# A gated cross-attention and sparse-FFN kernel on one core: direct factor writes, new instruction orders, a halved last tile

## What is computed

```python
x = x + tanh(g_xattn[0]) * xattn(layernorm(x), ctx, mask)
x = x + tanh(g_ffn[0]) * ffn(layernorm(x), w_gate, w_up, w_down)
...
def ffn(x, w_gate, w_up, w_down):
    h = silu(x @ w_gate) * (x @ w_up)        # 512 -> 2048
    h = keep_two_largest_of_each_four(h)     # by absolute value
    return h @ w_down                        # 2048 -> 512
```

## Time and profile before

| | |
|---|---|
| median of 3 runs | 1099.13 us (1098.95 to 1099.48) |
| the profiled execution | 1101.32 us, span 1099.5 us |
| PE busy | 1074.1 us (98%), 4960 matmuls |
| DVE, ACT, POOL busy | 796.6, 614.1, 222.2 us |
| mean granted PE clock | 0.995 |
| DMA | 254.75 MB, mean 232 GB/s |

### The profile page before, as it was taken

One profiled execution on the slowest core, in us unless ns is written; L12 is line 12 of the kernel. 1 busy time (PEld: TensorE's weight loads), 2 busy tenths in 40 slices (PEclk: granted clock), 3 DMA queues, 4 the chain that ended last, 5 costly groups with the idle time before them and its releaser, 6 DMA issues.

```text
span 1099.5 us, 15140 instructions
## 1 busy us (share of the span) xinstructions
PE 1074.1 (98%) x4960; PEld 879.7 (80%) x4960; DVE 796.6 (72%) x1391; ACT 614.1 (56%) x1126; POOL 222.2 (20%) x340
## 2 busy tenths in 40 slices
PE   7999899999997999999999999999999999999998
PEld 6888677888885888888888888878888888888886
DVE  6999789998985566675856666676757565665775
ACT  6999675777753444454545444444544444443452
POOL 6887312222111110001111111100011111111101
PEclk9999999999998999999999999999999999999999
DMA  8999985999898777788879777787798666767726
GB/s 299 324 308 329 357 320 130 326 316 289 278 287 272 228 198 201 202 276 207 227 237 324 171 186 187 179 275 202 237 292 243 153 155 156 192 153 192 197 29 134
DMA packets 89966, 254.75 MB, mean 232 GB/s; under 512 B 9121, under 2 KB 9633, under 8 KB 85537
## 3 DMA queue, kind: packets, MB, share of 16 engines
q1 hardware_dynamic: 68288, 205.55, 53.1%
q0 software_dynamic: 21600, 48.24, 25.5%
HBM read 154.14 MB, written 99.61 MB: 231 GB/s over the span
## 4 chain that ended last, share of the span: by engine, by line
PE 76%; DVE 5%; DMA 4%; ACT 1%; issue 1%; SPq 0%; DVEq 0%; ACTq 0%
PE ps_y L1365 10%; PE ps_y L1367 9%; PE ps_y L1366 9%; PE ps_a L1295 9%; PE ps_a L1299 9%; PE ps_a L1297 9%; PE ps_d L1295 5%; PE ps_d L1299 5%; PE ps_d L1297 5%; PE ps_c L1299 2%; PE ps_c L1295 2%; PE ps_c L1297 2%; DMA x_blk<-xnT_scratch 2%; DMA xm_scratch<-x_out 2%; DMA xm<-xm_scratch 1%
## 5 line engine op out<-in xcount | busy, mean ns | idle before, releaser
L612 POOL DMA_DIRECT2D out_rows<-y_out x124 | 105.6, 855 | 734.1 <-ACT y_out L760 730.4
L1295 PE MATMUL ps_a<-xm,w_ring 128*128 128x512 f32 x512 | 201.6, 394 | 11.6 <-DMA xm<-xm_scratch 7.8
L1297 PE MATMUL ps_a<-xm,w_ring 128*128 128x512 f32 x512 | 200.6, 392 | 0.0
L1299 PE MATMUL ps_a<-xm,w_ring 128*128 128x512 f32 x512 | 200.5, 392 | 0.0
L760 ACT ACTIVATE y_out<-ps_y,ffn_gate 128x512 f32<-128x512 f32 x124 | 85.2, 688 | 188.3 <-PE ps_y L1367 188.0
L1365 PE MATMUL ps_y<-dn,h_hi 128*128 128x512 f32 x480 | 188.1, 392 | 0.3 <-ACT y_out L760 0.2
L1367 PE MATMUL ps_y<-dn,h_lo 128*128 128x512 f32 x480 | 187.3, 390 | 0.0
L1366 PE MATMUL ps_y<-dn,h_hi 128*128 128x512 f32 x480 | 186.7, 389 | 0.0
L1295 PEld LDWEIGHTS ps_a<-xm,w_ring 128*128 128x128 f32 x512 | 96.6, 189 | 35.6 <-DMA xm<-xm_scratch 8.2
L737 ACT ACTIVATE h_hi<-hidden 128x512 fp32r<-128x512 f32 x128 | 73.1, 625 | 82.3 <-DVE hidden L1063 82.2
L1037 DVE TENSOR_TENSOR beats<-h_abs 128x512 bf16<-128x512 f32 x186 | 117.6, 683 | 1.3 <-ACT h_abs L730 1.3
(11 more groups left out here) (114 smaller groups left out, 1865.8 us busy)
## 6 DMA issues: line engine op xcount, KB each, us to landing
w_ring<-w_scratch SPq DMA_DIRECT2D x147, 512.0 KB, 4.4
out_rows<-y_out POOLq DMA_DIRECT2D x124, 256.0 KB, 4.2
w_scratch<-w_ring SPq DMA_DIRECT2D x56, 512.0 KB, 5.6
xm_scratch<-x_out SPq DMA_DIRECT2D x42, 512.0 KB, 5.8
xm<-xm_scratch SPq DMA_DIRECT2D x21, 1024.0 KB, 7.2
w_raw<-in_L_ffn_w_down SPq DMA_DIRECT2D x9, 1024.0 KB, 7.8
x_in<-in_x SPq DMA_DIRECT2D x32, 256.0 KB, 4.9
ctx_in<-in_ctx SPq DMA_DIRECT2D x32, 256.0 KB, 5.1
```

What stands on the lines that cost most here:

```text
L612: nc.gpsimd.dma_start(out[RING * (n // (2 * TILES * QS)) + TILES * ORDER[order] + n % TILES], y_out[:, n % 4], accum_op=ALU.add).then_inc( ...
L1295: nc.tensor.matmul(to, w_ring[:, k, e, 0, c], xm[:, k, 0, c], start=begins and c == 0, stop=False, skip_group_check=not begins)
L1297: nc.tensor.matmul(to, w_ring[:, k, e, 0, c], xm[:, k, 1, c], start=False, stop=False, skip_group_check=not begins)
L1299: last = nc.tensor.matmul(to, w_ring[:, k, e, 1, c], xm[:, k, 0, c], start=False, stop=c == 1, skip_group_check=not begins)
```

## The change

1. **Direct factors.** Factors 5 and 6 of half k = 1 for pair 1 (the last two) are written by ACT and DVE straight into `xm`, once the last unit of pair 0 has made product 2 or 6. They are not stored; `load_xm` for these two loads only half k = 0 (512 KB). SP's order is now 0 to 6.
2. **First four units.** `copy_a1(0, ·)` goes into slot 37 of ACT's attention loop; two raw pieces of unit 2 are loaded earlier by SP, one earlier by POOL; the orders of ACT and DVE in steps 0 and 1 are changed; the last `x_low` of pair 0 goes from POOL to DVE.
3. **The end.** The four `dn_low` of the last step go from DVE to POOL, ahead of its adding DMAs; one `h_low` moves ahead of the fourth `keep`; the compares of step 15 are done after the low parts.
4. **Last tile.** Its 12 matmuls of 512 columns become 24 of 256 in two groups, the second into the idle bank `ps_c0`; DVE adds and SP stores each half.

```diff
+DIRECT = ((1, 1, 5), (1, 1, 6))
-PIECE_AT = {..., 38: (2, 0)}
+PIECE_AT = {..., 36: (2, 0), 37: (2, 1)}
+def x_stores(m):
+    return m // 2 - (1 if m >= 14 else 0)
+LAST_ROWS = [(t, slice(0, D)) for t in range(TILES - 1)] + [(TILES - 1, slice(c, c + D // 2)) for c in (0, D // 2)]
...
# x_to, x_high
-            if p == 0:
+            if p == 0 or (p, k, i) in DIRECT:
                 return xm[:, X_TO[i], 0, k], xm[:, X_TO[i], 1, k]
+            if (p, k, i) in DIRECT:
+                act.wait_ge(made[X_TO[i]], 4 * QS * p)
...
# load_xm
+                    if (p, n // 7, n % 7) not in DIRECT:
+                        sp.wait_ge(x_out_stored[n % 2], 16 * (x_stores(14 * (p - 1) + n) + 1))
+                if (p, 1, X_AT[k]) in DIRECT:
+                    sp.dma_start(xm[:, k, :, 0].bitcast(F32), xm_dram[p - 1, k][:, :, 0]).then_inc(xm_loaded[k], 16)
+                    return
...
# PE, product
                         pe.wait_ge(xm_loaded[k], 16 * p)
+                        if (p, 1, X_AT[k]) in DIRECT:
+                            pe.wait_ge(x_lo_done, x_count(p, 1, X_AT[k]))
...
# SP
-            load_w_piece(sp, nc.sync, 2, 1)
-                        for k in range(PROD) if s >= QS else (0, 1, 3, 4, 5, 2, 6):
+                        for k in range(PROD):
-                                if s < QS and k == 2:
+                                if s >= QS and k == PROD - 1:
                                     x_stored_at(s, 2)
-                                if k == PROD - 1:
-                                    x_stored_at(s, 3 if s < QS else 2)
...
# POOL
-                if n - 1 in X0_AT:
+                if n - 1 in X0_AT and n < SLOTS - 2:
+            load_w_piece(pool, nc.gpsimd, 2, 2)
             for k in range(4):
                 pool.wait_ge(x1_stored[k], 16 * (B // 4))
...
             load_dn(0)
-            load_w_piece(pool, nc.gpsimd, 2, 2)
+                    if (s, half) == (LAST, 1):
+                        dn_low(pool, nc.gpsimd, s)
...
# ACT, slot 37
+                if n == SLOTS - 2:
+                    copy_a1(0, 0)
+                    copy_a1(0, 1)
# ACT, step 0
-                    copy_a1(0, 0)
-                    copy_a1(0, 1)
-                    w_high(act, 1, 2)
                     copy_d0(0, 0)
                     copy_d0(0, 1)
+                    w_high(act, 1, 2)
                     w_high(act, 1, 3)
                     spread(act, 2, 0)
                     w_high(act, 1, 4)
+                    w_high(act, 1, 5)
                     silu1(0, 0)
                     silu1(0, 1)
-                    w_high(act, 1, 5)
+                    spread(act, 2, 1)
...
                     w_high(act, 1, 6)
-                    spread(act, 2, 1)
                     copy_a0(1, 0)
-                    for j in range(GROUP):
-                        dn_high(0, j)
                     copy_a0(1, 1)
...
                     w_high(act, 2, 1)
+                    dn_high(0, 0)
+                    dn_high(0, 1)
                     copy_a1(1, 0)
                     copy_a1(1, 1)
+                    dn_high(0, 2)
+                    dn_high(0, 3)
# ACT, step 1: unit 2: copy_a1, h_high, copy_d0, silu0, x_high (silu0 was first); unit 3: copy_a1 ahead of absolute and silu0
...
# DVE, slot 37: x_low of the last factor; step 0:
+                    w_low(dve, nc.vector, 1, 5)
                     gated0(0, 0)
-                    w_low(dve, nc.vector, 1, 5)
...
-                    for i in range(4):
-                        w_sum(dve, 2, i)
+                    w_sum(dve, 2, 0)
+                    w_sum(dve, 2, 1)
                     add_c22(1, 0)
                     add_c22(1, 1)
+                    w_sum(dve, 2, 2)
+                    w_sum(dve, 2, 3)
                     w_low(dve, nc.vector, 2, 2)
+                    w_low(dve, nc.vector, 2, 3)
                     add_c12(1, 0)
+                    gated0(1, 0)
                     add_c12(1, 1)
...
# w_low(2, 6) and add_c11(2, ·) go from the end of step 0 (ahead of count_wins) to step 1, behind its four h_low
# DVE, the last step
-                if s == LAST:
-                    dn_low(s)
+                    keep(s, 0, kept_order(s)[:3])
+                    h_low(s, 0, kept_order(s)[0])
+                    keep(s, 0, kept_order(s)[3:])
-            compare(s, 1, ((0, 1), (2, 3)))
-            for j in kept_order(s):
+            for j in kept_order(s)[1:]:
                 h_low(s, 0, j)
-            compare(s, 1, REST)
+            compare(s, 1, ((0, 1), (2, 3)) + REST)
...
# PE, down
+                    for columns in [c for r, c in LAST_ROWS if r == t] if (s, order) == (LAST, 1) else (slice(0, D),):
+                        to = (ps_c[0] if columns.start else ps_y[n % 2])[:, columns]
+                            nc.tensor.matmul(to, h_hi[:, h, j, at], right[:, 0, j, columns], start=at_j == 0, stop=False)
```

More of the change, by code:

```diff
@@ L300, in load_x_blk, with dn_low @@
                          xnT_dram[p - 1].rearrange("p (a c) n -> p a c n", a=2)[:, :, k]).then_inc(x_blk_loaded, 16)
+        def dn_low(engine, instructions, s):
+            for j in range(GROUP):
+                raw, high, low = dn_places(s, j)
+                engine.wait_ge(dn_hi_done, GROUP * DN_BUILT.index(s) + j + 1)
+                instructions.tensor_tensor(low, raw, high.bitcast(F32), ALU.subtract).then_inc(dn_lo_done, 1)
         def spread_ready(engine, u, blk):
@@ L538, in _ @@
             sp.dma_start(rows[:], out.rearrange("b s d -> s b d")[:, b:b + TILES]).then_inc(rows_loaded, 16)
-            for t in range(TILES):
-                sp.wait_ge(y_added, t + 1)
-                sp.dma_start(out[b + t], rows[:, t]).then_inc(rows_stored, 16)
+            for i, (t, columns) in enumerate(LAST_ROWS):
+                sp.wait_ge(y_added, i + 1)
+                sp.dma_start(out[b + t][:, columns], rows[:, t, columns]).then_inc(rows_stored, 16)
             for k in range(4):
                 sp.wait_ge(y_stored[k], 16 * (2 * STEPS - 1))
-            sp.wait_ge(rows_stored, 16 * TILES)
+            sp.wait_ge(rows_stored, 16 * len(LAST_ROWS))
         @block.gpsimd
@@ L641, in copy_a0, with copy_a1 @@
                 nc.scalar.activation(cp[:, e, 0], ps_a[e][:], ACT.Copy).then_inc(a0_copied[e], 1)
+            def copy_a1(u, e):
+                act.wait_ge(made[2], 2 * u + e + 1)
+                wait(act, h1_done[e], u)
+                nc.scalar.activation(cp[:, e, 1], ps_a[e][:], ACT.Copy).then_inc(a1_copied[e], 1)
             for n in range(SLOTS):
@@ L793, in _ @@
                             h_high(0, 0, j)
+                        copy_d0(u, 0)
+                        copy_d0(u, 1)
+                        silu0(u, 0)
+                        silu0(u, 1)
+                        x_high_at(s, 0)
                     else:
@@ L897, in _ @@
                     spread(act, u + 1, 0)
+                if s == 1:
+                    copy_a1(u, 0)
+                    copy_a1(u, 1)
                 for j in first:
@@ L901, in _ @@
                 silu0(u, 1)
-                copy_a1(u, 0)
-                copy_a1(u, 1)
+                if s > 1:
+                    copy_a1(u, 0)
+                    copy_a1(u, 1)
                 if building:
@@ L1071, in h_low @@
                                         ALU.subtract).then_inc(h_lo_done, 1)
-            def dn_low(s, tiles=range(GROUP)):
-                for j in tiles:
-                    raw, high, low = dn_places(s, j)
-                    dve.wait_ge(dn_hi_done, GROUP * DN_BUILT.index(s) + j + 1)
-                    nc.vector.tensor_tensor(low, raw, high.bitcast(F32), ALU.subtract).then_inc(dn_lo_done, 1)
             def x_low_at(s, point):
@@ L1116, in _ @@
                         h_low(0, 0, j)
+                    w_low(dve, nc.vector, 2, 6)
+                    add_c11(2, 0)
+                    add_c11(2, 1)
                     add_c22(u, 0)
```

68 lines of the change are left out of this document (29 added, 39 removed).

## The result

The changed kernel takes 1085.06 us (median of 4 runs, 1082.77 to 1086.38) against 1099.17 (1098.95 to 1099.48): ratio 0.9869, 95% interval 0.9852 to 0.9887. That is 14.1 us less; 15.6 were forecast, and the median lies inside the range. The profiled execution took 1086.38 us with a span of 1084.6, so its gain (15.0 of span) is not that of the median either: executions of this kernel lie 3.6 us apart, those of the kernel before only 0.5 in this measurement (up to 4 in later ones).

A forecast was written before the change was run, and what follows sets the result against it. PE's matmul count was taken to bound nearly all FFN windows, so only PE's gaps could be won: 10.6 + 3.8 + 0.9 + 0.3 = 15.6 us, taking the median from 1099.13 to 1083.5, range 1080.0 to 1089.5.

The forecast's parts named there:

- Direct factors: Unit 8: PE's gap before product 2 and the slow matmuls behind it go, 10.6 us gained, bounds 5 and 10.6.
- The pace of 0.23 MB per us: Loads of `xm` for unit 8: 6 MB at this pace, the last landing at 346, all in time by 8 us or more.
- First four units: Units 0 to 3: gaps worth about 7.7 us, of which 3.8 taken as gain, bounds 0.5 and 7.
- `x1n`: First units, DVE: with `x_low` moved from POOL to DVE, `x1n` ends 0.9 us earlier and PE gets some 0.5.
- the gap at 171.81: PE's 1.24 us wait for `copy_d0(2,0)`; with three DVE operations moved behind, `keep` comes 1.8 us earlier.
- with it landed at 142: Unit 1: w_down's load lands at 142, `copy_d0(1,0)` is done at 148.3 and unit 2 starts 2.2 us earlier.
- The rival of this name, at most 1 us: First units give back their gain because w_down's or a raw piece's load ends last: 1086.5 us, chance 0.2.
- The end: Last step: PE's wait for `h_low`, some 1.2 us, closes; 0.3 comes back, so 0.9 us gained.
- so 0.3 comes back: Next `down` at the end: its first `h_low`, done at 1083.5, is wanted at 1083.2, so 0.3 us is lost again.
- Last tile: Last tile in halves: DVE's last operation gains 0.3 us, the store 0.1, matmuls cost 0.12; net gain 0.3.
- The rival of the slower side: Unit 1: ACT waits ahead of its first `x_high` for the store of `xnT`; landing at 155 gives 1102 us, chance 0.02.

The follow-up runs named there:

- the kernel with piece (2,1) behind it: Changed kernel with raw weight piece (2,1) loaded by SP behind the store of `xnT` instead of ahead of it: 1082.92 us, ratio 0.9847.
- the control: The changed kernel measured a second time with nothing edited: 1085.33 us, ratio 0.9868 to the kernel before.
- the kernel with unit 1's work put behind: Changed kernel with unit 1's `copy_a1`, `copy_d0` ahead of all `dn_high`, DVE's order likewise, and piece (2,3) ahead of w_down: 1085.60 us, ratio 0.9871.

## Why the prediction was right, point by point

- **Direct factors, 10.6 forecast, 10.60 measured** in two traces against the one trace from which the forecast was read, 10.0 by the medians of the part alone. All the sub-steps held: loads landed at 341.27 at the latest (forecast 346 in the time of the trace before, which is 343 here), no wait of ACT or PE for the direct writes, clock 1.00 through unit 8. The pace of 0.23 MB per us was conservative: 6 MB from 316.95 to 341.27 is 0.25. That the queue's order alone gives a bit over half was not in the forecast.
- **First four units, 3.8 forecast, 2.8 measured** (0.18 at product 1 of unit 0 to 2.97). This is the term that was mis-sized. `copy_a1` early gave 2.2 (0.72 to 2.89), as said; `x1n` took 0.54 us, so that step held too; the gap at 171.81 is gone. The step that failed is "with it landed at 142": the store of `xnT` landed 3.9 us later (the text itself allowed 3), so w_down at 143.75, and `copy_a1(1,0)` behind it cost PE 1.6 us. Unit 2 started 1.4 us earlier (1.61 less the 0.18 of before unit 0) and not 2.2, and units 2 and 3 kept 1.36 and not 1.6: together the 2.8. That the store is the cause is shown by the kernel with piece (2,1) behind it. The rival of this name, at most 1 us, was also right in its mechanism; the truth lay between the two.
- **The end, 0.9 forecast, 1.30 measured** (13.13 to 14.43; the same in the part alone). The gap closed for 1.24. The step "so 0.3 comes back" was wrong by a small size: it put the next `down` 10.9 us behind the start of this one (48 x 0.227), and it is 11.20 after and 11.27 before, since the matmuls of `down(15,0)` start 0.233 us apart on average in both traces, one like the other, and not 0.227. Why they do is not shown. The first `h_low` of `down(15,1)` was done 10.9 us behind, so that there was 0.3 to spare where 0.3 was expected to be missing. The Trainium skill's page SBUF — State Buffer, on the shared port pair, would have had DVE operations with two SBUF inputs shut out beside POOL's. POOL's four took 5.06 us here and ended by 1043.9, long before the end's work. The only DVE operations beside them (line 1043, at 1041.70 and 1043.06) read one input from PSUM and took 0.69 us, as before. The page is neither borne out nor refuted by that.
- **Last tile, 0.3 forecast, 0.53 measured** (0.56 in the part alone). Matmuls of 256 columns started 0.12 us apart, as taken:

```profile
1078.82 0.28 PE L1399 MATMUL ps_y<-dn_last,h_hi 128*128 128x256 f32 x1
1078.94 0.28 PE L1400 MATMUL ps_y<-dn_last,h_hi 128*128 128x256 f32 x1
1079.06 0.29 PE L1401 MATMUL ps_y<-dn_last,h_lo 128*128 128x256 f32 x1
```

  with weight loads still shown at 0.188 each and as close together as the matmuls, so they add nothing to the distance even where it is shorter than they are. By the rule of the Trainium skill's page TensorE: Matmul & The Clock Gate, under what overlaps and what doesn't, each would have added to the distance; the measurement decides against it for this form. DVE's last operation fell from 0.75 to 0.48 us (0.27), and the store with 128 KB landed 1.70 us after its issue instead of 2.0, where I had taken 0.1.
- **Not forecast: the second pair.** 0.7 us went between unit 12 and unit 16, because the `x_blk` load takes between 9.0 and 11.6 us from issue to landing in executions where nothing on that path was edited (9.67 in the kernel before, 10.37 after, 11.61 with the first units alone, 8.99 in the control), and PE's distance at product 5 of unit 12 follows it: 0.28, 0.98, 2.23, none (0.23). All ten traces that leave this path alone agree: 8.96, 8.99 and 9.28 us go with no gap, then 9.67, 9.79, 10.16, 10.37, 10.37, 10.76 and 11.61 with 0.28, 0.40, 0.77, 0.98, 0.99, 1.38 and 2.23. So each us of landing beyond some 9.6 is a us of PE. The size of the term is luck of the execution, and no edit tried here was shown to remove it at a gain.

Against the forecast sum, the terms by trace are 10.60 + 2.79 + 1.30 + 0.53 - 0.44 (what was lost between unit 12 and `down(14,1)`) = 14.8: the misses of the small terms, -1.0, +0.4, +0.2 and -0.44, explain 0.8 of the 1.5 us by which the median misses. The other 0.7 is of the size by which executions differ (the second measurement has 14.8 by medians and not 14.1). One reason can be named, though no run shows its share: the forecast took gains read from an execution 2.2 us slower than its median, with the largest unit 8 gap of four traces, off the median in full.

The rival of the slower side (ACT waiting ahead of `x_high` for the store of `xnT`) did show: ACT waited 1.37 us until 134.77. It cost nothing, as it was over before the 136 named.

## What to carry to other kernels

Where the last pieces of a large operand are made just before use, look whether they must take the way through DRAM at all: direct writing of two of fourteen made two stores and half of two loads unnecessary, and moving the store forward by three loads gave only a bit over half. When an operation is moved ahead, follow every transfer that shares its queue: one store with 1 MB more ahead of it landed 3.9 us later and gave unit 1 a new wait, and putting one 512 KB load behind it again was worth 2 us, where the reorderings tried on top of it gave nothing that can be told. And see a kernel's spread as information: two traces of the same kernel showed a wait that sits near an edge, where a load 1.4 us later against PE cost 4.3 us at first and 2.9 in the end.

## What the runs showed that was not expected

- A standstill of PE of 2.88 us, with everything before it at full clock, was followed by matmuls 0.43 us apart for 5.6 us (the 1.2 GHz level; granted clock 0.69 and 0.74 in the windows). Starts 2.32 us apart in unit 2 of the kernel with unit 1's work put behind were followed by distances of 0.31, 0.23, 0.24 and 0.27 and only then by seven of 0.43. Starts 1.86, 2.23 and 2.41 us apart in other traces (the last at 127.01 in the kernel before) were followed by one distance of 0.31 and then by 0.227. So the length of the gap alone does not decide whether a late load is paid once or twice, and these traces do not show what does.
- The same load (`x_blk`, 1 MB), at a place where the programs do not differ, lands 9.0 to 11.6 us after its issue; in two executions of the changed kernel alone it took 8.99 and 10.37.
- A DVE operation with one SBUF tensor input (line 962, line 991 after) took 1.44 us beside POOL's `x_low` and 0.54 without. It was held, not slowed: in all six cases of the kernel before in which POOL's operation had 0.35 us or more left to run, it ended 0.28 us behind POOL's end, whether it took 0.66 us or 1.44, and where POOL had 0.27 us or less left it took its usual 0.53 to 0.55. Two more of the kind (1.05 and 0.92 us, at 115.04 and 118.06) are still there in the kernel after; whether PE would gain by moving them was not tried.
